# Expert stage of a convolution and attention hybrid: the weight side of the first layer taken from a register instead of from two copies of the code behind a branch

## The reference

```
gate_probs = softmax(x @ gate_w.T)                # 8 experts
top_v, top_i = top_k(gate_probs, 2)
for e in range(8):
    h = silu(x @ w1[e] + b1[e])                   # 512 -> 2048
    y = h @ w2[e] + b2[e]                         # 2048 -> 512
    out = out + y * comb_w[..., e:e + 1]          # zero where e was not chosen
```

## Time and profile before

| | us |
|---|---|
| runs of the kernel before | 1468.13 and 1470.18 (median 1469.16) |
| the profiled execution, first to last instruction | 1469.3 |
| PE busy | 1237.3 (84%) |
| DVE, ACT, POOL busy | 1016.8, 761.8, 298.5 |
| first-layer matmuls (L2349) on the chain that ended last | 16% of the span |
| second-layer matmuls (L2370) on that chain | 15% of the span |

### The profile page before, as it was taken

The page is one execution under the profiler, slowest core; times in us unless marked ns, Lnnn a source line. Parts: engine busy times, 40 slices in busy tenths (PEclk is TensorE's granted clock), DMA queues, the critical chain, the costliest instruction groups (busy, mean ns, idle before and its releaser), DMA issues.

```text
span 1469.3 us, 33539 instructions
## 1 busy us (share of the span) xinstructions
PE 1237.3 (84%) x12366; PEld 848.8 (58%) x12367; DVE 1016.8 (69%) x1663; ACT 761.8 (52%) x1227; POOL 298.5 (20%) x363
## 2 busy tenths in 40 slices
PE   3735799998588999847489999768999999999996
PEld 2205576775466677423345555636677677767674
DVE  3668888888788888869567667475567755476432
ACT  2236577677666767622643424424466655375331
POOL 0121223332222333422000000034111111111111
PEclk9766999999899999979599999658999999999998
DMA  4043000003200000320220000328347564446111
GB/s 147 1 155 123 13 5 5 5 3 115 69 12 6 5 4 4 104 119 11 97 115 0 0 0 0 134 107 254 136 143 250 191 201 136 143 168 219 24 26 22
DMA packets 38129, 120.26 MB, mean 82 GB/s; under 512 B 9960, under 2 KB 14184, under 8 KB 28080
## 3 DMA queue, kind: packets, MB, share of 16 engines
q1 hardware_dynamic: 32416, 107.28, 20.3%
q0 software_dynamic: 5648, 12.13, 4.1%
HBM read 105.61 MB, written 12.76 MB: 81 GB/s over the span
## 4 chain that ended last, share of the span: by engine, by line
PE 47%; DVE 4%; ACT 2%; issue 2%; POOL 0%; POOLq 0%; DVEq 0%; ACTq 0%
PE banks L2349 16%; PE banks L2370 15%; PE banks L1880 7%; PE banks L1910 3%; PE banks L2319 1%; PE banks L2302 1%; PE banks L1936 1%; PE banks L2336 1%; PE banks L1949 1%; ACT ab_wi_hi L1749 1%; PE banks L2295 1%; PE banks L1959 1%; DVE f_qa L1418 0%; PE banks L1933 0%; ACT ab_un L1783 0%
## 5 line engine op out<-in xcount | busy, mean ns | idle before, releaser
L2349 PE MATMUL banks<-eb_x_hi,eb_w_hi 128*128 128x128 f16 x1344 | 228.7, 220 | 4.7 <-DVE eb_w_lo L2229 4.7
L2349 PE MATMUL banks<-eb_x_lo,eb_w_hi 128*128 128x128 f16 x1344 | 228.6, 220 | 0.0
L2349 PE MATMUL banks<-eb_x_hi,eb_w_lo 128*128 128x128 f16 x1344 | 228.6, 220 | 0.0
L1118 PE MATMUL banks<-mb_u_hi,mb_wi_hi 128*128 (+3 forms) x1088 | 190.7, 221 | 12.4 <-ACT mb_ca L845 10.7
L1118 PE MATMUL banks<-mb_u_hi,mb_wi_lo 128*128 (+3 forms) x1088 | 190.4, 221 | 0.0
L1118 PE MATMUL banks<-mb_u_lo,mb_wi_hi 128*128 (+3 forms) x1088 | 190.2, 221 | 0.0
L2229 DVE TENSOR_TENSOR eb_w_lo<-eb_raw,eb_w_hi 128x2048 f32 (+1 forms) x64 | 142.6, 2287 | 23.0 <-ACT eb_w_hi L2235 16.0
L647 DVE SCALAR_TENSOR_TENSOR mb_ca<-mb_xp,mb_par,mb_ca 128x128 f32<-128x128 f32 x384 | 149.5, 451 | 5.2 <-ACT mb_ca L845 3.4
L2349 PEld LDWEIGHTS banks<-eb_x_hi,eb_w_hi 128*128 128x128 f16 x1344 | 132.4, 99 | 7.4 <-issue 5.1
L2349 PEld LDWEIGHTS banks<-eb_x_lo,eb_w_hi 128*128 128x128 f16 x1344 | 132.4, 98 | 2.4
L2349 PEld LDWEIGHTS banks<-eb_x_hi,eb_w_lo 128*128 128x128 f16 x1344 | 132.4, 99 | 0.0
(11 more groups left out here) (441 smaller groups left out, 2842.6 us busy)
## 6 DMA issues: line engine op xcount, KB each, us to landing
eb_raw<-e_w SPq DMA_DIRECT2D x64, 1024.0 KB, 6.0
mb_ring<-m_in_w SPq DMA_DIRECT2D x8, 1072.0 KB, 6.5
ab_raw<-a_in_w SPq DMA_DIRECT2D x4, 1154.0 KB, 9.0
mb_ring<-m_out_w SPq DMA_DIRECT2D x4, 1024.0 KB, 5.3
xcm<-x_cm SPq DMA_DIRECT2D x4, 512.0 KB, 5.1
t_res<-x_tm SPq DMA_DIRECT2D x1, 2048.0 KB, 8.9
t_kept<-t_res SPq DMA_DIRECT2D x8, 256.0 KB, 2.0
mb_wi_hi<-t_kept SPq DMA_DIRECT2D x1, 2048.0 KB, 9.2
```

The lines of the kernel that those rows point to most:

```text
L1118: x = e.matmul(ps[0:width, bank, n * P:(n + 1) * P], a[:, k, f:f + width], b[:, k, ds(i * P, P)], start=(k == 0 and m == 0), stop=(k == KD ...
L2349: o = e.matmul(ps[:, j, c * P:(c + 1) * P], a[:, side, k, f * P:(f + 1) * P], b[:, k, :], start=(k == 0 and m == 0), stop=(k == KD - 1 and ...
```

## The change

The two copies of `layer1` and the branch between them go. One copy stays, and the weight operand takes its side from the register:

```diff
@@ layer1
                     for k in range(KD):
                         for m, (a, b) in enumerate(((w_hi, x_hi), (w_hi, x_lo), (w_lo, x_hi))):
-                            o = e.matmul(ps[:, j, c * P:(c + 1) * P], a[:, side, k, f * P:(f + 1) * P], b[:, k, :],
+                            o = e.matmul(ps[:, j, c * P:(c + 1) * P],
+                                         a[:, ds(side, 1), k, f * P:(f + 1) * P].rearrange("p o c -> p (o c)"), b[:, k, :],
                                          start=(k == 0 and m == 0), stop=(k == KD - 1 and m == 2))
@@ block
-            with e.If(side < 1):
-                layer1(s, 0)
-            with e.Else():
-                layer1(s, 1)
+            layer1(s, side)
```

## The result

The changed kernel takes **1540.8 us** (median of 2 runs, 1540.03 to 1541.57) against 1469.16 us: ratio **1.0473**, 95% interval 1.045 to 1.0496. It is slower by 4.7%. The profiled span is 1538.2 us against 1469.3, so 68.9 us came on top.

The account below looks back on a forecast made before the run. The prediction took PE to bound the kernel, with its sequencer setting the changed first layer's pace. From 1469.3 us, +74 for blocks 1 to 20, -4.4 in block 16 and -7.6 in block 0 gave 1531 us, range 1512 to 1565.

Parts of the forecast that it names:

- PE bounds, and its sequencer within it: Expert layers: PE sets the time; in the changed first layer its sequencer (0.24 us a triple) outlasts the array (0.167 us).
- The lead of 17: First layer: the sequencer runs 17 matmuls ahead of the array, so the other 175 of 192 go at its pace.
- The rival of twice that: First layer: a lead of 34 matmuls, +2.3 us per block with the hand-over, 1503 us in all; chance 0.03.
- The pace: First layer: three matmuls with two register instructions take the sequencer 0.24 us; 14.3 us in place of 10.7, +3.6 per block.
- The hand-over: From first layer to second: the sequencer's way to the next matmul outlasts the 0.44 us of transposes, +0.1 us per block.
- The jump's holes: Blocks 0 and 16: idle pieces of 6.88 and 2.52 us behind first jumps over the second copy go; -7.6 and -4.4 us.
- the case that the prediction mentions, late code that only moves the hole: Blocks 0 and 16: if code is fetched late even without a jump, the gains of 7.6 and 4.4 us are nil.
- What is late next: Block 1: the gather for block 2 lands at 1026.9 us, just as block 1's first layer ends, so it just fits.
- the rival of hidden register work: First layer: the array keeps its 10.72 us and only the idle pieces go, 1457 us, 0.8% faster; chance 0.07.
- The clock: From block 1 on: granted clock stays 1.00; the rival, a fall to 1.2 GHz in the first layer, 1647 us, chance 0.04.

Follow-up runs that it names:

- the two kernels that show that case: Changed kernel with one weight address per block, 1464.56 us; changed kernel with one register instruction per triple, 1464.15 us.
- the second kernel with additions: Kernel before plus two register additions per triple of the first layer, kept by using their last value once per group of 48: 1574.94 us.

## Why the prediction was right

**PE bounds, and its sequencer within it: right.** The steady block is still PE's own work. With one register instruction the array sets the pace and with two the sequencer does, and the kernels with one address (register operands, hardly any register instructions) and with additions (register instructions, static weight addresses) show that it is the instructions that count.

**The lead of 17: right.** It was read from one place, and the kernel with groups 0 and 2 by register shows 96 - 79 = 17 after the lead was spent and rebuilt. The rival of twice that is out. The Trainium skill ("Advanced Engine Details and Errata", section "Engine Queue Depths") gives TensorE a queue depth of 64; the runs show 34 instructions both times.

**The pace: right.** 0.244 us a triple for 0.24 forecast, from the nearest place of the same form. The first layer grew by 3.77 us in place of 3.6. The hand-over was mis-sized, +0.19 us a block for +0.1, in part by rounding (0.5 + 0.1 - 0.44 is 0.16). With the lead spent, the register instruction and the wait ahead of the transposes lie open: from the last matmul of the first layer to the first transpose it is 0.25 us (1053.59 to 1053.84), 0.06 before; the transposes themselves follow each other as before. Together 3.96 for 3.7, +79.2 us for +74.

**The price of one register instruction.** The prediction took the pace of a triple from rows and needed no price for one instruction; the runs give it. Triples with one, two and three register instructions take the sequencer about 0.13, 0.244 and 0.377 us, so each holds it for 0.12 to 0.13 us, though its recorded duration is 0.03 to 0.05 us, and the six pushes add nothing that shows. The Trainium skill ("Runtime: NRT & Kernel Launch", section "Instruction fetch mechanics") names an issue floor of some 20 cycles per instruction; the prediction's estimate from it, 0.13 us for a triple with two register instructions, is about half of the 0.244 us measured.

**The jump's holes: right in size, a little large; the reason only in part.** Both went: -6.6 us for -7.6 in block 0, -3.8 for -4.4 in block 16. What was left out is that a first pass through new code is a little slower even without a jump: block 16 takes 0.59 us more than a steady block, and block 0 came out 1.0 us over its forecast. The prediction put the holes down to the first jump. The kernel with four branches has three quick first jumps for each slow one, and the kernel with group 0 by register has a hole in straight code. So the case that the prediction mentions, late code that only moves the hole, was nearer than it looked: that the changed kernel has no hole is measured, but the prediction had only half of the reason, and why this kernel is spared was not tried.

**What is late next: right, by a little.** PE waited for nothing after 1000 us, and the gather for block 2 fitted: issued at 1022.8 us, it landed 3.7 us later, some 2 us before its transposes at 1028.36. Where the first layer stayed at 10.7 us it did not: 5.2 us of waiting. So the rival of hidden register work was priced too low: the two kernels that show that case ran in 1464.56 and 1464.15 us, where the prediction had 1457.

**The clock: right.** 1.00 from block 1 on, even with a first layer of 21.97 us.

Sum: +69 us for +62 forecast. The size that was off is the block, by 0.26 us times 20, and the two holes, by 1.6 us.

## What to carry to other kernels

Before addressing an operand through a register, count the register instructions per matmul group and hold their time on the sequencer, 0.12 to 0.13 us each in these runs with the pushes inside it, against the array's time for that group. With 512 columns a triple takes the array 0.65 us and two of them vanish; with 128 columns it takes 0.167 us and two are one too many. What counts is the number of distinct addresses, not of register operands. A branch around static copies costs nothing in steady state while the sequencer has a lead; its price here is a hole of some microseconds the first time through a body of the loop.

## What the runs showed that was not expected

- A register-addressed weight load costs nothing by itself (10.7 us for a first layer with 192 of them and one register pair), and two additions that no weight address uses cost as much as two address computations (0.253 and 0.244 us a triple).
- Two, four or six pushes behind a register instruction make no difference: the next one starts 0.124 us after a FUSED_REGOPS in all three cases.
- Some first jumps took 2.7 to 7.7 us and others 0.18 to 0.39 us. Cutting the copies into quarters made the long one in block 0 shorter (7.7 to 3.3 us) and that in block 16 longer (3.4 to 4.3 us). In the kernels before, with four branches and with group 0 by register, each long jump, and the one hole without a jump, ended 1.3 to 1.5 us after a 16 KB packet of the instruction queue (2.0 and 1.4 us in the second kernel with additions). In the changed kernel such packets run as well and no hole stands beside them.
